# A decoder layer with experts: the branches over the last routed tiles, before and after a change of their grouping

## What is computed

```python
scores = sigmoid(xf @ gate_w.T)                      # T = 2048 tokens, E = 16 experts
biased = scores + expert_bias
# of four groups of experts the best two stay, of their experts each token takes the best TOPK = 4
w = take_along_axis(scores, idx, axis=1); w = w / sum(w)
h = silu(einsum('td,edh->teh', xf, w1)) * einsum('td,edh->teh', xf, w3)     # h = 352
y = einsum('teh,ehd,te->td', h, w2, cw)
z = silu(xf @ sw1) * (xf @ sw3) @ sw2                # the shared expert, twice 352 wide
return layernorm(x + y + z)
```

## Time and profile before

| what | value |
| --- | --- |
| median of 3 runs | 1550.25 us |
| the three runs | 1549.85, 1560.35 and 1550.25 us |
| the profiled execution, its own time | 1557.36 us |
| span of its trace, first to last instruction | 1555.6 us |
| mean granted clock of TensorE | 0.931 of full |
| first silg of the routed tiles' last group to the last silg (tiles 71 to 74) | 1501.44 to 1521.50 us |
| last matmuls of the experts end | about 1524 us |

### The profile page before, as it was taken

How to read it: one execution, slowest core, us unless ns; L and a number is a source line. 1 busy time by engine, 2 the same in 40 slices (tenths; PEclk the granted TensorE clock), 3 DMA queues, 4 the chain that set the end, 5 groups by cost and what they waited for, 6 DMA issues and landing times.

```text
span 1555.6 us, 24674 instructions
## 1 busy us (share of the span) xinstructions
PE 1392.0 (89%) x7587; PEld 1024.2 (66%) x7595; DVE 909.2 (58%) x1574; ACT 418.6 (27%) x628; POOL 342.0 (22%) x294
## 2 busy tenths in 40 slices
PE   7998998999998999948987998999999999878991
PEld 3454455445453445437876887899999989767881
DVE  2442787568855886678654886434343355464534
ACT  1132132402332133321111101323232234343423
POOL 3000000000100010040000383244343344343332
PEclk9979998899979997969998999999999999988996
DMA  8521433225321622320410101544664455767347
GB/s 264 141 73 41 149 85 94 69 76 143 82 54 44 190 69 69 131 70 23 144 55 14 41 31 45 161 84 80 138 136 78 78 136 133 227 177 225 59 76 240
DMA packets 90127, 164.28 MB, mean 106 GB/s; under 512 B 8544, under 2 KB 29536, under 8 KB 89968
## 3 DMA queue, kind: packets, MB, share of 16 engines
q1 hardware_dynamic: 73168, 122.88, 25.5%
q0 software_dynamic: 16816, 39.59, 13.7%
HBM read 113.42 MB, written 49.02 MB: 104 GB/s over the span
## 4 chain that ended last, share of the span: by engine, by line
PE 47%; issue 36%; DVE 7%; DMA 5%; POOL 2%; ACT 1%; SPq 1%; ACTq 0%; DVEq 0%; POOLq 0%
PE psUA L1010 12%; PE psUB L1010 11%; PE psY L1017 8%; PE psR L1017 4%; PE psTX L993 2%; PE psR L1116 2%; PE psTH L1026 2%; DMA room<-in_L_ffn_w_dram 2%; POOL xr L804 1%; PE psST L1206 1%; DMA xr<-in_x_dram 1%; DVE x L1496 1%; ACT w_s L864 1%; PE psOT L1225 1%; PE psR L1065 1%
## 5 line engine op out<-in xcount | busy, mean ns | idle before, releaser
L1010 PE MATMUL psUA<-w_s,xgT 128*128 (+1 forms) x1284 | 249.8, 346 | 8.5 <-issue 7.2
L1010 PEld LDWEIGHTS psUA<-w_s,xgT 128*128 128x128 f32 x1284 | 218.6, 200 | 16.5 <-issue 14.7
L1010 PE MATMUL psUB<-w_s,xgT 128*128 (+1 forms) x1284 | 226.0, 325 | 0.0
L1010 PEld LDWEIGHTS psUB<-w_s,xgT 128*128 128x128 f32 x1284 | 212.2, 191 | 0.0
L834 POOL DMA_INDIRECT sx_d<-yg,dst_i x74 | 119.5, 1614 | 311.1 <-ACT yg L913 278.1
L873 ACT ACTIVATE silg<-psUA 128x352 f32<-128x352 f32 x107 | 49.7, 464 | 455.1 <-PE psUB L1010 455.1
L1017 PE MATMUL psY<-w_s,hgT 128*128 (+3 forms) x621 | 160.5, 403 | 0.5 <-issue 0.5
L1590 DVE TENSOR_REDUCE nm<-psR 128x1 f32<-128x128 f32 (+3 forms) x256 | 114.6, 487 | 68.9 <-PE psR L1194 64.1
L1411 DVE SCALAR_TENSOR_TENSOR hg<-silg,cws,psUB 128x352 f32<-128x352 f32 x75 | 43.4, 579 | 181.1 <-ACT silg L873 181.1
L1017 PEld LDWEIGHTS psY<-w_s,hgT 128*128 128x128 f32 (+1 forms) x621 | 113.2, 190 | 21.9 <-issue 1.0
L1116 PE MATMUL psR<-xT,room 128*128 128x512 f32 x256 | 121.2, 622 | 2.4 <-ACT xT L923 2.4
(11 more groups left out here) (225 smaller groups left out, 2102.8 us busy)
## 6 DMA issues: line engine op xcount, KB each, us to landing
room<-in_L_ffn_w_dram SPq DMA_DIRECT2D x32, 704.0 KB
scr_d<-qhl SPq DMA_DIRECT2D x32, 512.0 KB, 3.7
qst<-scr_d SPq DMA_DIRECT2D x48, 256.0 KB, 3.9
kst<-scr_d SPq DMA_DIRECT2D x48, 256.0 KB, 5.8
room<-in_L_ffn_w_dram SPq DMA_DIRECT2D x16, 512.0 KB
xt<-in_x_dram SPq DMA_DIRECT2D x5, 1024.0 KB, 7.6
xr<-in_x_dram SPq DMA_DIRECT2D x4, 1024.0 KB, 5.5
breg<-in_fside_BxS2xS_dram SPq DMA_DIRECT2D x4, 1024.0 KB, 8.0
```

The costliest lines, as they stand in the source:

```text
L1010: mm = pe.matmul(t[:, 0:F], xgT[:, par, a_, c * P:(c + 1) * P], w[:, buf, b_, c, :], start=(c == 0 and n == 0), stop=(c == C - 1 and n == ...
```

## The change

The groups are of two tiles (63 and 64, 65 and 66, ... 77 and 78, and 79), nine in place of five. The branches are nested: the branch over group g + 1 stands at the end of the body of group g, so that a group that isn't run skips all that follow. The flag of the next group is loaded at the head of a group's body and carried in a register to the branch; that of group 0 is loaded before step 62. The values of the next tile are loaded in the middle of every step, the last one of a group and step 62 among them, and are carried over the branch; on PE those of the tile before are carried too. The four engines use one function `tiles` for this; on POOL there is no state to carry but the flag. The tables of flags have 16 places in place of 8.

```diff
--- before.py
+++ after.py
@@ -436,8 +436,8 @@
         hi_f = se("hi_f", [P, NT, TOPK])
         need_f = se("need_f", [P, RT])
 
-        run_f = se("run_f", [P, 8])
-        run_i = se("run_i", [1, 8], I32)
+        run_f = se("run_f", [P, 16])
+        run_i = se("run_i", [1, 16], I32)
         runs_f = se("runs_f", [P, 1])
         fin_f = se("fin_f", [P, 2])
         fin_i = se("fin_i", [1, 1], I32)
@@ -528,35 +528,31 @@
 
 
         MUST = TOPK * T // P
-        GROUP = 4
+        GROUP = 2
         GSTART = MUST - 1
         NG = (RT - GSTART + GROUP - 1) // GROUP
         assert (TOPK * T + (P - 1) * E) // P < RT and GSTART <= MUST
         assert GSTART + (NG - 1) * GROUP == RT - 1
 
-        def runs(eng, g):
-            return eng.If(eng.value_load(run_i[0:1, g:g + 1], min_val=0, max_val=1))
-
-        def tiles(eng, body):
-
-            for j in range(GSTART):
-                body(j, j % 2)
-            for g in range(NG):
-                with runs(eng, g):
-                    for j in range(GSTART + GROUP * g, min(RT, GSTART + GROUP * (g + 1))):
-                        body(j, j % 2)
-
-        def tiles_ahead(eng, body):
-
-            def span(lo, hi):
-                facts = tile_facts(eng, lo)
-                for j in range(lo, hi):
-                    facts = body(j, j % 2, facts, j + 1 < hi)
-
-            span(0, GSTART)
-            for g in range(NG):
-                with runs(eng, g):
-                    span(GSTART + GROUP * g, min(RT, GSTART + GROUP * (g + 1)))
+        def run_flag(eng, g):
+            return eng.value_load(run_i[0:1, g:g + 1], min_val=0, max_val=1)
+
+        def tiles(eng, body, state=None):
+
+            def group(g, flag, state):
+                with eng.If(flag):
+                    lo, hi = GSTART + GROUP * g, min(RT, GSTART + GROUP * (g + 1))
+                    following = run_flag(eng, g + 1) if g + 1 < NG else None
+                    for j in range(lo, hi):
+                        state = body(j, j % 2, state)
+                    if g + 1 < NG:
+                        group(g + 1, following, state)
+
+            for j in range(GSTART - 1):
+                state = body(j, j % 2, state)
+            flag = run_flag(eng, 0)
+            state = body(GSTART - 1, (GSTART - 1) % 2, state)
+            group(0, flag, state)
 
         UP, DOWN = [0, 1], [2]
 
@@ -834,7 +830,7 @@
                 pool.indirect_dma_start(sx_d, bass.IndirectOffsetOnAxis(ap=dst_i[:, j:j + 1], axis=0),
                                         yg[:, par, :], None, compute_op=ALU.add).then_inc(s_sca, 16)
 
-            def one(j, par):
+            def one(j, par, _):
                 if j + 2 < RT:
 
                     pool.wait_ge(s_tx, j + (NT + 1))
@@ -890,12 +886,12 @@
                     act.wait_ge(s_dn, NH - 1)
                     split(SH, 0, DOWN)
 
-            def one(j, par, facts, ahead):
+            def one(j, par, facts):
                 if_first(act, facts, split, UP)
                 gate(j + NH)
                 if not is_last(j, RT):
                     high_x(j + (NT + 1), 1 - par)
-                after = tile_facts(act, j + 1) if ahead else None
+                after = tile_facts(act, j + 1) if j + 1 < RT else None
                 if not is_first(j):
                     evacuate(j - 1, 1 - par)
                 if is_first(j):
@@ -968,7 +964,7 @@
 
 
             shared(act, half)
-            tiles_ahead(act, one)
+            tiles(act, one, tile_facts(act, 0))
 
             for n in range(NT):
                 act.wait_ge(s_cn, n // FG + 1)
@@ -1080,8 +1076,9 @@
                 pe.wait_ge(s_w2lo, regs[0])
                 down(psY[par], bass.ds(regs[1], 1))
 
-            def one(j, par, before, regs, ahead=True):
-
+            def one(j, par, state):
+
+                before, regs = state
 
                 pe.wait_ge(s_wlo, regs[0] * 2)
                 pe.wait_ge(s_xe, j + (NT + 1))
@@ -1090,26 +1087,11 @@
                     gathered(j + 1, 1 - par)
                 if is_first(j):
                     down_shared(NT - 1, SH - 1, 1 - par)
-                after = registers(j + 1) if ahead else None
+                after = registers(j + 1) if j + 1 < RT else None
                 if not is_first(j):
                     down_routed(j - 1, 1 - par, before)
                 turned(j + NH)
-                return after
-
-            def routed():
-
-                def span(start, par, n):
-                    before, regs = registers(start - 1), registers(start)
-                    for k in range(n):
-                        before, regs = regs, one(start + k, (par + k) % 2, before, regs, k < n - 1)
-
-                before, regs = None, registers(0)
-                for j in range(GSTART):
-                    before, regs = regs, one(j, j % 2, before, regs, j < GSTART - 1)
-                for g in range(NG):
-                    start = GSTART + GROUP * g
-                    with runs(pe, g):
-                        span(start, start % 2, min(GROUP, RT - start))
+                return regs, after
 
             def product(out_, pairs):
                 for n, (l, r) in enumerate(pairs):
@@ -1261,7 +1243,7 @@
 
 
             shared(pe, half, between)
-            routed()
+            tiles(pe, one, (None, registers(0)))
 
         @block.vector
         def _(dve):
@@ -1442,14 +1424,14 @@
                 if is_last(n, NT) and s == SH - 1:
                     split(SH, 0, DOWN)
 
-            def one(j, par, facts, ahead):
+            def one(j, par, facts):
                 if_first(dve, facts, split, UP)
                 weighted(j)
                 if not is_last(j, RT):
                     low_x(j + (NT + 1), 1 - par)
                 if is_first(j):
                     summed(NT - 1, 1 - par)
-                after = tile_facts(dve, j + 1) if ahead else None
+                after = tile_facts(dve, j + 1) if j + 1 < RT else None
                 turned(j + NH)
                 if_first(dve, facts, split, DOWN)
                 return after
@@ -1680,7 +1662,7 @@
 
 
             shared(dve, half, between)
-            tiles_ahead(dve, one)
+            tiles(dve, one, tile_facts(dve, 0))
 
             cc = [0]
 
```

## The result

Over 18 runs each the median went from 1556.14 us before (1548.86 to 1562.40) to 1547.74 us after (1545.50 to 1551.96). The measured ratio is 0.9955 with a 95% interval of 0.9939 to 0.9972: 7.0 us faster, between 4.4 and 9.5 (the two medians taken alone lie 8.4 us apart). The forecast was 10.5 us faster, 1539.7 us, and "within 1%". The sign is right and 1547.74 lies in the forecast range, but the gain is two thirds of the forecast, which lies outside the interval, and the median is 8.0 us above the forecast time. Of these 8.0 us, 5.9 come from the starting point: I subtracted from 1550.25 us, the median of three runs, and the median of 18 runs of the same kernel is 1556.14. And 18 runs tell apart much less than the 1% that I had called the limit: this change is clear of noise.

A forecast was written before the change was run, and what follows sets the result against it. PE, busy 89% of the span, was taken to bound the kernel, stalling at group heads; 3.81 + 3.80 + 2.9 = 10.5 us off the 1550.25 us median gave 1539.7 us, range 1532 to 1551.

The forecast's parts named there:

- within 1%: Whole kernel: time after the change within 1% of the time before, given a chance of 0.84.
- Number of tiles: Routed stage: 74 needed tiles, so tiles 0 to 74 still run, 75 steps, and no step goes away.
- Heads: First tiles of old groups, 63, 67 and 71: without PE's four loads they gain 3.81, 2.9 and 3.80 us.
- The cover and its sum: PE between hg and the next weight load: 1.17 us of sequencer work hides under 1.48 us of queued matmuls.
- Added heads cost nothing: New group starts at tiles 65, 69 and 73: branch and flag load, 0.73 us on PE, stay hidden.
- rival of stalling heads: Group heads on PE: each still stalls, six in place of three, 11.4 us more, 1561.7 us; chance 0.05.
- 3.81 us = 1.98 stall + about 1.8 at the lower clock.: Old head of tile 63 on PE: 1.98 us of stall, about 1.8 at the lower clock and in restart.
- Five flags become nine in DVE's table work: shorter than a row can show.: DVE's filling of the flag tables: nine flags in place of five cost less than a profile row can show.
- Sum: Whole kernel: gains of 3.81, 3.80 and 2.9 us at tiles 63, 71 and 67 make 10.5 us.
- What I forecast is the median, 1550.25 - 10.5 = 1539.7 us.: Whole kernel: forecast time, the earlier median of 1550.25 us less the gain of 10.5; chance 0.76.
- only the stall goes: Group heads on PE: the lower clock stays or turns up elsewhere, gain about 5.4 us, 1544.9 us; chance 0.10.
- Resolution: Whole kernel: about 1% is what a measurement can tell from no change, against a forecast of 0.68%.

The follow-up runs named there:

- e12: Changed kernel with ACT and DVE loading their three values again behind each branch, PE still carrying; steps 67 and 68 took 8.24 and 10.42 us.
- the three doses: Changed kernel with one, two or four unused extra loads on PE at each group's head; one added 0.28 to 0.33 us, two 0.94 to 1.04, four brought 10.5 us steps.
- e3: Changed kernel with no branch over groups and no flag loads, tiles 0 to 74 written out; tiles 62 to 74 82.63 us, ratio 0.9953 to the kernel before.
- e5: Kernel before with only the two flag tables widened from 8 to 16 places; 5.3 us slower than the kernel before (2.2 to 8.4).
- e6: Changed kernel with groups of four and flag tables of 8 places; 10.6 us faster than the kernel before (7.0 to 14.3), ratio 0.9932.
- e4: Kernel before, unchanged, traced a second time; tiles 62 to 74 took 92.72 us, plain step 6.69 us.
- e2: Kernel before with groups of two and tables of 16 places, values loaded again behind each branch; 14.6 us slower than the kernel before (9.5 to 19.7).
- e10: Changed kernel with two more unused loads on PE at each of the six heads; they added 0.94 to 1.04 us at heads away from tile 67.

## Why the prediction was right and where it was not

- **Number of tiles.** Right: 75 steps and 74 scatters, the same tiles.
- **Heads.** Right: 10.50 and 10.49 us became 6.75 and 6.74; at 67 and 68 the gain is 2.9 us as forecast. There the forecast put the gain down to PE's stall alone; e12 shows that ACT and DVE had to carry their values too. Between tiles 62 and 74 the gain is 9.62 us; with 12 steps x 0.04 us and the stall of 0.44 us at tile 74 given back it is 10.5, the forecast sum.
- **The cover and its sum** (1.17 against 1.48, 0.65 a load). Right, by the three doses: 0.3, 1.0 and, with the lower clock, 3.8 us at a head. A load took 0.30 us on PE, and two loads instead of one added 0.65. The Trainium skill, page DMA: Bandwidth & Descriptors, section Latency and other measured facts, gives a floor of about 600 ns for such a load, which this trace does not bear out.
- **Added heads cost nothing.** Right, by e3: no branch at all saves nothing in the steps. The rival of stalling heads falls with it.
- **"3.81 us = 1.98 stall + about 1.8 at the lower clock."** Right for the traced execution; two of the six heads 63 and 71 of such kernels kept the clock and cost 2.3 us. On the sum this does little: tiles 62 to 74 took 92.72 us in both traces of before, since tile 67 was slower in the second, and 91.87 in e5, some 1.5 us less than 92.72 with 12 steps x 0.06 us added. As a mean over the three traces that takes about 0.5 us off the gain, an estimate from three traces.
- **"Five flags become nine in DVE's table work: shorter than a row can show."** This is the step that failed. I priced the wider tables by the instructions that fill them, and not by what stands behind them in SBUF, and so put their cost at nothing. They move the split weights by 64 bytes and make each plain step 0.04 us longer, an estimated 3.2 us over 75 steps; alone, in e5, they cost 5.3 us (2.2 to 8.4).
- **Sum.** -10.5 + 3.2 + 0.5 for the clock's chance = -6.8, where -7.0 (-9.5 to -4.4) was measured. The closeness is in part luck, since each term is uncertain by a microsecond or so.
- **"What I forecast is the median, 1550.25 - 10.5 = 1539.7 us."** This failed as a starting point: the median of three runs was 5.9 us below that of 18 (1556.14). From the better one the forecast would have been 1545.6. That 1546.9, forecast for the profiled execution, is near the measured 1547.28 is in part luck, since it lacks the tables' 3 us.
- **The rival "only the stall goes".** Its gain of 5.4 us lies in the measured interval, so the time does not exclude it; the trace does. No lower clock stands behind any head (1.00 over 1428 to 1511 us), and no pause but one of 0.26 us at tile 67, whose step is as long in e3, without a branch.
- **Resolution.** I took 1% for what can be told from no change, and so gave 0.84 to "within 1%" with a change of 0.68% in hand. That was too coarse: with 18 runs each the interval is 0.33% wide, and a ratio of 1 lies outside it.

## What to carry to other kernels

Between two steps of a pipelined loop, add up what the sequencer does from the last wait to the first engine instruction, and set it against what the engine's queue still holds: here registers and branches were free up to a cover of 1.48 us, beyond it a load cost its full 0.65 us, and a pause of 2.0 us became 3.8 through the clock at most heads. Carry values over a branch rather than load them behind it, first of all on the engine that bounds. When an edit resizes a tensor, look at what is allocated behind it: compare the plain steps of the two kernels, far from the edit, before explaining the total; here carrying with groups of four, whose five flags need no wider tables (e6), has the best ratio, 0.9932 of the kernel before, though its interval overlaps that of the changed kernel.

## What the runs showed of the hardware that I had not expected

- The time of matmuls changed slightly with how far in SBUF the moving weights lie from the tensors allocated ahead of them: plain steps of 6.69, 6.77, 6.73 to 6.75, 6.73, 6.73 and 6.69 us with the weights moved by 0, 32, 64, 96, 128 and 256 bytes, and 6.69 us with all tensors from xg to the weights moved together by 64.
- The clock behind a pause of about 2 us came out both ways: after 2.04 us it was 1.00 in e4, while psUA took 3.0 to 3.5 us after the same pause in e2; after 1.98 and 2.07 in the first trace of before it was 0.59 and 0.56; in e10 it was 1.00 after 0.70 and 1.58 us.
- Skipped branches on PE took 3.09 and 3.78 us in the kernel before and 5.17 us in the changed kernel, where one jump skips all that is left; entered ones took 0.066 to 0.083. The skipped ones stand behind PE's last tile, so they cost nothing on the path.
